# A decoder layer on one core: the 16-bit part of the attention probabilities is made by ACT instead of POOL

## The reference

```python
x = x + attn(layernorm(x), w_qkv, w_out)
#   qkv = x @ w_qkv;  scores = causal(q @ k.T / 8);  p = softmax(scores);  out = (p @ v) @ w_out
x = x + xattn(layernorm(x), ctx)
x = x + ffn(layernorm(x))
```

## Time and profile before

| | us |
|---|---|
| median of 3 runs | 2787.72 |
| lowest and highest | 2785.35, 2791.86 |
| the profiled execution | 2785.46 |
| its span, first to last instruction | 2783.6 |

### The profile page before, as it was taken

The page is one execution under the profiler, slowest core; times in us unless marked ns, Lnnn a source line. Parts: engine busy times, 40 slices in busy tenths (PEclk is TensorE's granted clock), DMA queues, the critical chain, the costliest instruction groups (busy, mean ns, idle before and its releaser), DMA issues.

```text
span 2783.6 us, 37859 instructions
## 1 busy us (share of the span) xinstructions
PE 2415.4 (87%) x14389; PEld 1187.7 (43%) x14389; DVE 1877.4 (67%) x3421; ACT 783.4 (28%) x1557; POOL 711.4 (26%) x981
## 2 busy tenths in 40 slices
PE   0588889699889999879979999979989999978996
PEld 0233444344444444445444444444444444434453
DVE  4577877646866767755785777765685777765566
ACT  1033333322213333321212333332211343332110
POOL 3123433214311222212421222212430222221220
PEclk9899999899999999989999999989989999998997
DMA  6678788857636776785654777776663677775543
GB/s 178 214 174 184 164 208 181 204 126 151 141 94 126 141 150 135 136 213 120 137 115 105 153 135 146 143 183 138 143 142 88 133 142 143 143 156 145 106 84 83
DMA packets 986009, 403.97 MB, mean 145 GB/s; under 512 B 937116, under 2 KB 946332, under 8 KB 985828
## 3 DMA queue, kind: packets, MB, share of 16 engines
q1 hardware_dynamic: 985828, 401.56, 65.3%
HBM read 133.05 MB, written 33.55 MB: 60 GB/s over the span
## 4 chain that ended last, share of the span: by engine, by line
PE 52%; DVE 22%; DMA 12%; issue 5%; ACT 4%; POOL 3%; SPq 2%; ACTq 0%; POOLq 0%; DVEq 0%
PE ps_p L532 8%; PE ps_p L534 8%; PE ps_p L533 8%; DMA r<-pn 7%; PE ps_s L532 5%; PE ps_s L533 5%; PE ps_s L534 5%; PE ps_s L577 5%; DVE pn L813 4%; PE ps_o L602 4%; DVE peak L850 3%; ACT probs L739 2%; DMA qk<-in_x 2%; DVE bn L818 2%; PE ps_s L582 1%
## 5 line engine op out<-in xcount | busy, mean ns | idle before, releaser
L1077 POOL TENSOR_SCALAR pn<-probs,rden 128x640 f16<-128x640 f32 (+7 forms) x512 | 386.6, 767 | 1297.0 <-DVE rden L862 830.4
L739 ACT ACTIVATE probs<-ps_s,low,back 128x640 f32<-128x640 f32 (+7 forms) x512 | 421.3, 826 | 859.0 <-DVE low L853 747.7
L813 DVE SCALAR_TENSOR_TENSOR pn<-probs,rden,pn 128x640 f16<-128x640 f32 (+7 forms) x512 | 473.9, 958 | 159.7 <-POOL pn L1077 159.5
L532 PE MATMUL ps_p<-r,w 128*128 128x512 f16 x1344 | 513.1, 382 | 3.3 <-DVE qk L813 3.3
L533 PE MATMUL ps_p<-r,w 128*128 128x512 f16 x1344 | 512.1, 381 | 0.0
L534 PE MATMUL ps_p<-r,w 128*128 128x512 f16 x1344 | 511.9, 381 | 0.0
L577 PE MATMUL ps_s<-qk 64*128 64x512 f16 (+3 forms) x2304 | 242.1, 336 | 129.5 <-ACT probs L739 122.8
L850 DVE TENSOR_REDUCE peak<-ps_s 128x2 f32<-128x1280 f32 (+3 forms) x128 | 241.3, 1885 | 36.6 <-PE ps_s L582 33.9
L602 PE MATMUL ps_o<-r,vn 128*64 128x512 f16 (+3 forms) x2304 | 212.2, 340 | 36.7 <-issue 36.1
L532 PE MATMUL ps_s<-r,pn 128*128 128x512 f16 x512 | 200.1, 391 | 11.0 <-DMA pn<-pn 11.0
L577 PEld LDWEIGHTS ps_s<-qk 64*128 64x128 f16 x2304 | 91.0, 96 | 274.0 <-ACT probs L739 171.6
(11 more groups left out here) (163 smaller groups left out, 3545.7 us busy)
## 6 DMA issues: line engine op xcount, KB each, us to landing
w<-w_pairs SPq DMA_DIRECT2D x72, 512.0 KB, 4.0
qk<-in_x SPq DMA_DIRECT2D x32, 512.0 KB, 4.2
r<-wo_pairs SPq DMA_DIRECT2D x16, 1024.0 KB, 6.1
w_raw<-in_x SPq DMA_DIRECT2D x32, 512.0 KB, 4.7
out<-r SPq DMA_DIRECT2D x32, 512.0 KB, 2.9
r<-in_w_qkv SPq DMA_DIRECT2D x24, 512.0 KB, 5.6
w_raw<-in_w_qkv SPq DMA_DIRECT2D x24, 512.0 KB, 5.7
w_pairs<-w SPq DMA_DIRECT2D x24, 512.0 KB, 5.5
```

What stands on the lines that cost most here:

```text
L532: pe.matmul(ps, lh, rh, start=start and k == ks[0], stop=False)
L739: act.activation(probs_part(q, j, w), ps_s[:, j, scores(q)], ACT.Exp, bias=low[:, n % 2, i:i + 1], scale=sc, accum_out=den[:, n % 2, i:i + ...
L813: dve.scalar_tensor_tensor(out=to, in0=bank, scalar=scale, in1=rounded, op0=ALU.mult, op1=ALU.subtract).then_inc(ok, 1)
L1077: pool.tensor_scalar(to, src, scale, 1.0, ALU.mult, ALU.mult).then_inc(ok, 1)
```

## The change

The 16 `H` steps of each pair leave POOL's list and stand in ACT's list, two tiles' exponentials later at most: `H00 H01` behind `E10 E11`, `H10 H11` behind `E20 E21`, and so on, `H70 H71` last. They are an ACTIVATE (Identity with the scale rden) in place of a TENSOR_SCALAR, with the same waits and the same semaphore. POOL keeps the splitting of the weights. `walk` is altered so that a once-only step can hang behind a name with its "+", because `VH` must now hang behind `WH2+`.

```diff
 ACT_BODY = """
-    E00 E01 CH21 E10 E11 E20 E21 CH00+ E30 E31 OH1- E40 E41 CH01+ E50 E51 CH10+ OH0 E60 E61 CH11+ E70 E71
-    CH20+
+    E00 E01 CH21 E10 E11 H00 H01 E20 E21 H10 H11 CH00+ E30 E31 H20 H21 OH1- E40 E41 H30 H31 CH01+ E50 E51 H40 H41
+    CH10+ H50 OH0 H51 E60 E61 CH11+ H60 H61 E70 E71 CH20+ H70 H71
...
 POOL_BODY = """
-    WH2+ H00 H01 H10 H11 H20 H21 H30 H31 H40 H41 WH0++ H50 H51 H60 H61 WH1++ H70 H71
+    WH2+ WH0++ WH1++
...
-    ONCE["POOL", pair, "H31"] = f"VH{u} VH{v}"
+    ONCE["POOL", pair, "WH2+"] = f"VH{u} VH{v}"
...
+                    elif kind == "H":
+                        q, j = a
+                        Q, i, w = TB * n + q, 2 * q + j, (q + 1) * P
+                        act.wait_ge(r_ok, Q + 1)
+                        if Q >= 2:
+                            act.wait_ge(t_in[q % 2], 16 * (Q // 2))
+                        if p == 0 and q < 2 and b > 0:
+                            act.wait_ge(xm_ok, TB * b)
+                        act.activation(pn_part(q, j, 0, w), probs_part(q, j, w), ACT.Identity,
+                                       scale=rden[:, n % 2, i:i + 1]).then_inc(h_ok, 1)
...
-                    elif kind == "H":
-                        q, j = a
-                        Q, i, w = TB * n + q, 2 * q + j, (q + 1) * P
-                        pool.wait_ge(r_ok, Q + 1)
-                        if Q >= 2:
-                            pool.wait_ge(t_in[q % 2], 16 * (Q // 2))
-                        if p == 0 and q < 2 and b > 0:
-                            pool.wait_ge(xm_ok, TB * b)
-                        rounded(pn_part(q, j, 0, w), probs_part(q, j, w), rden[:, n % 2, i:i + 1], h_ok)
```

More of the change, by code:

```diff
@@ L74 @@
 ACT_TAIL = """
-    E00 E01 CH21 E10 E11 KH E20 E21 JH0 E30 E31 OH1- E40 E41 QH0 JH1 E50 E51 OH0 E60 E61 QH1 JH2 E70 E71 QH2 JH3
-    QH3 LX0 OH1 CE0 LX1 CE1 CE2 CE3 LX2 CE4 CE5 CE6 CE7 AX0+ AX1+ AX2+ TX0 LX3 AX3+ TX1
+    E00 E01 CH21 E10 E11 H00 H01 KH E20 E21 H10 H11 JH0 E30 E31 H20 H21 OH1- E40 E41 H30 H31 QH0 JH1 E50 E51 H40 H41
+    OH0 E60 E61 H50 H51 QH1 JH2 E70 E71 H60 H61 QH2 JH3 H70 H71 QH3 LX0 OH1 CE0 LX1 CE1 CE2 CE3 LX2 CE4 CE5 CE6 CE7 AX0+ AX1+ AX2+ TX0 LX3 AX3+ TX1
     LX4 AX4+ GE0 TX2 WHI0 LX5 AX5+ GE1 TX3 WHI1 LX6 AX6+ GE2 TX4 WHI2 LX7 AX7+ GE3 TX5 WHI3 GE4 TX6 WHI4
@@ L80 @@
 POOL_TAIL = """
-    H00 H01 H10 H11 H20 H21 H30 H31 H40 H41 H50 H51 H60 H61 H70 H71 LS0 LH0 CHI0 LS1 CHI1 LH1 LS2 CHI2 CHI3 LS3
+    LS0 LH0 CHI0 LS1 CHI1 LH1 LS2 CHI2 CHI3 LS3
     CHI4 CHI5 LS4 CHI6 LS5 CHI7 LS6 AS0+ AS1+ AH0+ LS7
@@ L314, in walk @@
                         rest(kind, args, b + off)
-                    if off == 0:
-                        for once, which, _ in steps(ONCE.get((engine, n, kind + "".join(map(str, args))), "")):
-                            rest(once, which, 0)
+                    at = kind + "".join(map(str, args)) + ("+" * off if off > 0 else "-" * -off)
+                    for once, which, _ in steps(ONCE.get((engine, n, at), "")):
+                        rest(once, which, 0)
         def rows(j):
```

## The result

The changed kernel took 2897.44 us (median of 4 runs, 2890.48 to 2899.53) against 2788.57 us for the kernel before on the same chips. The ratio is 1.0387, 95% interval 1.0368 to 1.0406: 3.9% slower. Forecast were 2936 us, with a range from 2860 to 3005. The profiled execution was the fastest of the four (2890.48 us); its span is 2888.7 us, 105.1 more than before.

A forecast was written before the change was run, and what follows sets the result against it. PE, busy 87%, was taken as the bound, with two loops close behind. Inner pairs 85.5, clock 27, first pairs 5, sequence 0 15 and tails 16 made 148.5 us, giving 2936 us; range 2860 to 3005.

The forecast's parts named there:

- The mechanism: On ACT, the places of the moved H steps cost time, not their sizes: +4.75 us per inner pair before the clock.
- first loop: From M1- over T0, H20, L20 and exponentials to S5: OH1- waits behind H20/H21, S5 comes 2.6 us later.
- rows to look for: Changed profile: pair 52 to 55 us, OH1- behind H20's DMA wait, PE waits 2.6 and some 3 us, 1.0 us rests, half clock.
- second loop: From tile 4's exponentials over L30/L31, X5, X6 to S7: H30/H31 now follow those exponentials; S7 +4.75 us, including 2.6 at S5.
- The size of H: Each H on ACT, from the row with two register columns: 0.71, 0.81, 0.92, 1.03 us for 384 to 768 columns.
- sign of being wrong: H taking much less than 0.7 us for 384 columns, T0 landing by 950, or PE's wait at S5 under 1 us.
- The clock: PE's new waits ahead of S5 and S7 bring a half clock: 1.5 us a pair, between 0 and 2.9, 27 us in all.
- Rival 3: The half clock comes in each pair at S7: 18 x 1.4 us more, others 10 x 2; 2980 us; chance 0.2.
- Sequence 0, first pairs, tails: Outside the inner pairs: sequence 0 +15 us, three first pairs +5 (1.7 each), four tails +16 (4 each).
- Rival 1: DVE is relieved and that counts: faster, at most 1.6 us a pair, 34 us off, 2754 us; chance 0.05.
- Rival 2: Only the first loop shows, DVE's relief eats the second: some 2.2 us a pair, 2853 us; chance 0.15.
- Rival 4: The move changes nothing, as ACT's idle time takes it all: within 0.2% of 2788 us; chance 0.03.

The follow-up runs named there:

- Experiment 1: The changed kernel with OH1- ahead of H20 and H21 on ACT, in body and tail; ratio 1.0178 to the kernel before.
- E60: Not a run but a step of the kernel: the first of tile 6's two exponentials on ACT, between X6 and S7.
- E61: Not a run but a step of the kernel: the second of tile 6's two exponentials on ACT, between X6 and S7.
- experiment 4: The changed kernel with a column of zeros as bias of each H, which changes no value; ratio 1.0469 to the kernel before.
- experiment 2: The kernel before, all H on POOL, with one wait added: OH1- on ACT also waits until H21 is done; ratio 1.0286.
- experiment 3: The changed kernel with one projection quarter (P101+) ahead of S5 instead of behind it on PE; ratio 1.0450 to the kernel before.
- Experiment 9: The kernel before with H of tiles 1, 6 and 7 on ACT in the bodies, tails as before; ratio 0.9961, 2777.7 us.

## Why the prediction was right, and what was off

**The mechanism and both loops** are as forecast. From the end of M1- to S5: 9.5 us forecast, 9.1 measured (1070.65 to 1079.73), 6.9 before. From S5 to S7: 16.6 forecast, 16.2 measured, 14.4 before. Together 3.9 more, less 0.1 between S7 and M1-, is the 3.8 us that a pair grew, where 4.75 was forecast. Experiment 1 shows that the first loop's share comes from the place of one step. Of the rows to look for, four are there: H20 waits 2.30 us for `r<-pn` with OH1- behind it, PE waits 2.35 us ahead of S5, the rests of 768 columns take 1.01 us, and the half clock comes in part of the pairs. Two are not as named: the pair takes 51.1 us and not 52 to 55, and PE's wait ahead of S7 is 0.90 or 2.53 us and not some 3.

**What was misread without harm.** The 0.80 us that PE waited ahead of S7 was not the second loop's. DVE's X6 had waited 1.00 us for PE, and S5 to S7 was 14.44 us in all 18 inner pairs: the wait was PE's own S6, then X6 and E60/E61. So that loop had slack left before the change; in the changed kernel X6 follows L50 without a wait for PE. The sum goes from start to start along the changed order and doesn't use the reading. ACT's idle time would hold POOL's high parts five times, not four, and the first of the two VL waited 1.19 us in one of the pairs 3 to 6 and 0.74 in the others.

**The size of H was the first term off.** I took the row with two register columns, 1.239 us at 1024 columns. H has one, and took 1.140; 0.606 instead of 0.71 at 384, a little way towards what the prediction had named as a sign of being wrong. By experiment 4, 0.1 us a step is 0.55 us a pair, which is most of the 0.95 that was too much. The Trainium skill would have had it: ScalarE: Activation LUTs, What ACT_TABLE_LOAD costs, gives an ACTIVATE 186 ns + 0.833 ns an element and some 93 ns for each column operand. An estimate by the page is 0.60 us at 384 columns with one column operand and 0.69 with two; the trace agrees with 0.606 and 0.698.

**The clock was the second, and a step that failed.** The waits came (2.35 us) and the half clock with them, behind S5 in 15 of the 18 inner pairs. I charged 1.5 us a pair, 27 in all. In 14 of the 15 it cost nothing. Two pairs of the changed kernel, S7 behind a stretch at half clock (above: S5 at 1079.73, S7 at 1095.90, wait 0.90) and one at the full clock:

```profile
2396.69 1.15 PE L577 MATMUL ps_s<-qk 64*128 64x512 f16 x12 [2.35 <-ACT probs L739]
...
2412.86 1.47 PE L577 MATMUL ps_s<-qk 64*128 64x512 f16 x12 [2.53 <-ACT probs L739]
```

```profile
1079.00:1086.00 7.00, 6.27 (x30) 2.69 (x31) 4.14 (x7) 3.82 (x8) 0.00 (x0) 0.76 0.71 131
...
2396.00:2403.00 7.00, 6.31 (x38) 2.88 (x38) 4.13 (x7) 3.82 (x8) 0.00 (x0) 1.00 0.71 131
```

S5 to S7 is 16.17 us in both; PE's loss of 1.6 us only eats its wait ahead of S7. In one pair (S5 at 2293.41) the clock was half for longer, 0.55 over the 7 us, and S7 came 17.3 us after S5: there it cost 1.1 us, the only cost in these pairs. The text of the prediction had said that a half clock behind S5 hides, and then charged half a clock anyway because it expected the wait at S7 to be 3.0 us: it was 0.9 where the clock had fallen at S5 and 2.5 where it hadn't, and didn't bring the half clock there. Where the second loop isn't late (experiment 2) the half clock costs 1.1 us in the pair shown, and behind S7 (experiments 3 and 4) some 1.5. Rival 3 did not come in any pair of sequences 1 to 3.

**Sequence 0, first pairs, tails**: +11.3 with the earlier first pair (forecast 15), +4.7 (5), +21.1 (16). That the last two come near is in part luck. S5 to S7 grew by 0.9, 0.4 and 0.9 us in the three first pairs, 2.2 in all; nearly all of the other 2.5 came where the half clock and the wait ahead of S4 fell in sequence 2's. The tails were only read at X5, X6 and QH2; H10 behind the context's weights wasn't seen.

So the sum was 148.5 us where the traces show 105.1: the clock took 26 of the difference, the two loops in the inner pairs 18, sequence 0 another 4, and the tails gave 5 back.

**Rival 1** had its premises right, but for one size: rests of 768 columns take 1.01 us, no kernel here won more than 0.4 of the 1.6 us a pair, and DVE is 89 us less busy, though only 69 of these are the rests, for which 86 was forecast (0.822 us each, not 0.79); the rest lies in other steps, 13 us of it in `low`. Experiment 9 gets 0.35 us a pair of it by leaving tiles 0 and 2 to 5 on POOL, so that OH1- isn't delayed. **Rival 2** had a wrong mechanism: S5 to S7 grew by 1.8 us, so the second loop does show. **Rival 4** is out by the ratio.

**First pairs of 43.7 or 45.2 us.** They occur in most kernels here, the one before among them (45.1, 43.8 and 45.2 in sequences 1, 2, 3), and not only with tile 1 on ACT. The clock tells them apart. The first 7 us of such a pair, before the change, in sequence 1 and in sequence 2 (columns as in the earlier trace rows):

```profile
840.00:847.00 7.00, 5.78 (x27) 2.36 (x26) 4.22 (x16) 3.60 (x12) 2.50 (x6) 0.76 0.76 168
...
1496.00:1503.00 7.00, 5.78 (x37) 2.37 (x36) 4.47 (x17) 3.60 (x12) 2.15 (x5) 1.00 0.78 171
```

In the longer one the clock was granted half for a part, and it costs some 1.4 us. Why it falls in some sequences and not in others stays open.

## What to carry to other kernels

An engine that is idle for 70% of the time isn't free: ask of each step that is moved onto it what stands behind it there, and whose wait it brings along. Here 52 of 105 us came from one wait for a DMA ahead of a step of 0.6 us that had no part in it. And a cost such as the half clock has to be charged where it falls: where another loop makes PE wait behind it anyway, it is free (experiment 3's pairs of 51.1 us), and where PE is last it is not (experiment 2).

## What the runs showed of the hardware

- ACT's time falls by 0.09 us for each register column that an ACTIVATE doesn't need: 1.239 (two), 1.140 (one), 1.053 us (none) for 1024 columns from SBUF.
- A rest on DVE with two inputs in SBUF, 896 columns, took 1.49 us with POOL's high parts beside it and 1.15 us with ACT's. ACT's own time didn't suffer from DVE: H of 1024 columns took 1.13 us where such a rest ran beside it for more than half of it and 1.14 where none did.
- Waits of PE of one length, 2.35 us, were followed by a half clock in some pairs and not in others: the granted clock over the 7 us from S5 on was 0.76 or 1.00. The same holds of waits of 2.78 us ahead of S7 in experiment 4.
